# Attention and mixture-of-experts kernel: the softmax division moved from the probabilities to each pair's output, with an fp32 output product

## The reference

```
q = l2norm(q) * q_scale
k = l2norm(k) * k_scale
sim = einsum('bhid,bhjd->bhij', q, k) * SCALE + slopes * bias
sim = where(causal, -neg, sim)
attn = softmax(sim, axis=-1)
out = einsum('bhij,bhjd->bhid', attn, v)
out = out.transpose(0, 2, 1, 3).reshape(b, n, h * dh)
return out @ Wout
```

## Time and profile before

| | us |
|---|---|
| median of 3 runs (550.72 to 552.13) | 552.09 |
| the profiled execution, its own time | 550.33 |
| its span, from the first to the last instruction | 548.2 |
| start of step 4 of batch 0 / of batch 1 | 194.30 / 237.82 |
| one batch of the loop, step 4 to step 4 | 45.88 to 45.90 |
| step 4 of batch 6 to that of batch 7 | 44.08 |
| step 4 of batch 7 to the end | 36.86 |

### The profile page before, as it was taken

How to read it: one execution, slowest core, us unless ns; L and a number is a source line. 1 busy time by engine, 2 the same in 40 slices (tenths; PEclk the granted TensorE clock), 3 DMA queues, 4 the chain that set the end, 5 groups by cost and what they waited for, 6 DMA issues and landing times.

```text
span 548.2 us, 12299 instructions
## 1 busy us (share of the span) xinstructions
PE 431.0 (79%) x2867; PEld 318.0 (58%) x2868; DVE 413.8 (75%) x1468; ACT 365.9 (67%) x1097; POOL 320.1 (58%) x488
## 2 busy tenths in 40 slices
PE   0573334987889788997998998899799889889885
PEld 0472222766667566765765765576576566667663
DVE  3865713554455289989889998898899899899885
ACT  1451214565556687895886888689588788868864
POOL 2223778940000278957867886795886788678140
PEclk9996757799999999998998999999899999989999
DMA  8930111222221100000000100100000010010010
GB/s 220 352 109 21 48 43 54 57 60 59 61 62 57 31 0 15 8 1 21 21 0 10 29 0 0 29 10 0 19 19 0 4 34 0 0 29 10 3 39 10
DMA packets 28586, 21.17 MB, mean 39 GB/s; under 512 B 3560, under 2 KB 25744, under 8 KB 28432
## 3 DMA queue, kind: packets, MB, share of 16 engines
q1 hardware_dynamic: 25696, 16.65, 10.3%
q0 software_dynamic: 2048, 4.20, 2.5%
q10 hardware_dynamic: 816, 0.03, 0.1%
HBM read 12.48 MB, written 8.39 MB: 38 GB/s over the span
## 4 chain that ended last, share of the span: by engine, by line
POOL 29%; issue 22%; PE 20%; DVE 17%; ACT 4%; DMA 3%; POOLq 1%; SPq 1%; DVEq 1%; ACTq 0%
POOL rnorm L418 6%; POOL slot_x L408 6%; POOL arena_b L498 5%; POOL rpow L421 5%; PE bank L945 4%; DVE arena_b L894 3%; DVE arena_b L878 3%; PE bank L1152 3%; POOL pnull L487 3%; PE bank L947 3%; PE bank L946 3%; DMA arena_b<-in_L_ffn_wu_dram 2%; PE bank L1123 2%; PE bank L1131 2%; PE bank L1076 2%
## 5 line engine op out<-in xcount | busy, mean ns | idle before, releaser
L652 ACT ACTIVATE arena_b<-arena_b,nmx 128x130 f32<-128x130 f32 (+1 forms) x256 | 115.2, 458 | 29.3 <-DVE nmx L894 20.3
L878 DVE TENSOR_SCALAR arena_b<-arena_b,rden 128x130 f32<-128x130 f32 (+1 forms) x256 | 104.6, 454 | 4.6
L894 DVE CUSTOM_DVE_ANT_0 arena_b<-bank,bias 128x130 f32<-128x130 f32 (+1 forms) x256 | 81.0, 354 | 17.1 <-PE bank L1076 9.1
L1076 PE MATMUL bank<-arena_a 64*128 64x130 f32 (+1 forms) x512 | 59.7, 352 | 23.7 <-DVE nmx L894 22.7
L421 POOL TENSOR_TENSOR rpow<-ssm,mhalf 128x8 f32<-128x8 f32 x32 | 52.8, 1649 | 40.6 <-DVE ssm L859 40.6
L1067 PE MATMUL bank<-ident,arena_b 128*128 128x128 f32 x384 | 67.2, 284 | 7.0 <-DVE arena_b L878 7.0
L434 POOL TENSOR_TENSOR arena_b<-arena_b,rnorm 128x512 f32<-128x512 f32 x64 | 67.1, 1048 | 8.4 <-POOL rnorm L424 3.8
L590 ACT ACTIVATE arena_b<-bank 128x512 f32<-128x512 f32 x64 | 38.2, 597 | 32.0 <-PE bank L947 31.3
L418 POOL TENSOR_TENSOR rnorm<-ssm,mhalf 128x8 f32<-128x8 f32 x32 | 52.4, 1639 | 7.6 <-DVE ssm L859 7.6
L855 DVE TENSOR_REDUCE ssq<-arena_b 128x8 f32<-128x512 f32 x64 | 43.4, 678 | 16.0 <-ACT arena_b L590 15.9
L1076 PEld LDWEIGHTS bank<-arena_a 64*128 64x128 f32 x512 | 33.6, 186 | 36.5 <-DVE nmx L894 30.5
(11 more groups left out here) (203 smaller groups left out, 1128.1 us busy)
## 6 DMA issues: line engine op xcount, KB each, us to landing
slot_x<-probT SPq DMA_DIRECT2D x4, 640.0 KB, 7.7
arena_b<-slot_x SPq DMA_DIRECT2D x40, 64.0 KB, 1.8
slot_y<-arena_b SPq DMA_DIRECT2D x40, 64.0 KB, 1.6
arena_b<-in_L_ffn_wd_dram SPq DMA_DIRECT2D x1, 1024.0 KB, 10.3
arena_b<-in_L_attn_Wkv_dram SPq DMA_DIRECT2D x1, 1024.0 KB, 8.5
arena_b<-in_L_attn_x_dram SPq DMA_DIRECT2D x8, 128.0 KB, 2.1
out_dram<-arena_b SPq DMA_DIRECT2D x8, 128.0 KB, 1.8
arena_b<-in_L_attn_Wq_dram SPq DMA_DIRECT2D x1, 512.0 KB, 6.4
```

The lines of the kernel that those rows point to most:

```text
L652: sc.activation(prob[:, h % 4, c], sim[h % 2][:, c], ACT.Exp, scale=-1.0, bias=nmx[:, h % HEADS, t:t + 1], accum_out=den[:, h % HEADS, t:t ...
L878: ve.tensor_scalar(pr, pr, rden[:, h % HEADS, t:t + 1], None, ALU.mult).then_inc(g.pn, 1)
L894: ve.tensor_tensor_reduce(out=sim[h % 2][:, c], in0=bank[h % 2][:, c], in1=bias[:, c], scale=-SLOPES[h], scalar=3e38, op0=ALU.add, op1=ALU ...
L1076: ins = te.matmul(bank[half][:, c0:c1], qT[r, h // 2, q0:q0 + P], kT[r, h // 2, 0:c1 - c0], start=True, stop=True)
```

## The change

The probabilities stay as the exponential leaves them. For each pair of heads (odd h):

- DVE takes one reciprocal for both heads, in step h+2, and no longer multiplies (16 reciprocals and 32 multiplications of a batch become 8 reciprocals).
- POOL, in step h+2 and behind the norms of that step, spreads the reciprocals of the pair over a 128x256 tile `rwide`. It then multiplies the null columns by them where it copied before.
- PE, in step h+3 and behind the transposes of the probabilities, waits for it (`rw`) and transposes `rwide` into `rpair`, the other half of bank 4. It waits there for `odone` of the pair before as well.
- ACT, in step h+3, copies `rpair` to `rows` (it no longer reads `opair` in step h+5).
- DVE, in step h+5, multiplies `opair` by `rows` into `oT` (fp32).
- PE, in step h+6, uses one fp32 product in place of three fp32r products. `wo` is loaded as it is, its split in the prologue goes.

The diff, cut to its core:

```diff
@@ POOL, entry
                     if h is not None and h % 2:
                         p = h // 2
-                        pool.wait_ge(g.pn, TB * (HEADS * b + h + 1))
+                        pool.wait_ge(g.rd, PAIRS * b + p + 1)
+                        if part != "first" or p >= 2:
+                            pool.wait_ge(g.rps, PAIRS * b + p - 1)
+                        settled(pool)
+                        gp.tensor_copy(rwide[p % 2][:].rearrange("p (t h d) -> p t h d", t=TB, d=DH),
+                                       rden[:, 2 * (p % PAIRS):2 * (p % PAIRS) + 2, :].rearrange("p h t -> p t h").unsqueeze(3)
+                                       .to_broadcast([P, TB, 2, DH])).then_inc(g.rw, 1)
...
-                            gp.tensor_copy(pnull[:, t, 4 * q:4 * q + 4].rearrange("p (h n) -> p h n", n=2),
-                                           two[:, :, c0:c0 + NNULL]).then_inc(g.pnc, 1)
+                            gp.tensor_tensor(pnull[:, t, 4 * q:4 * q + 4].rearrange("p (h n) -> p h n", n=2),
+                                             two[:, :, c0:c0 + NNULL], bc(rden[:, 2 * q:2 * q + 2, t], NNULL),
+                                             ALU.mult).then_inc(g.pnc, 1)
@@ ACT, entry
-                    h = head_at(part, s, 5)
-                    if h is not None and h % 2:
-                        p = h // 2
-                        act.wait_ge(g.pvd, PAIRS * b + p + 1)
-                        if part != "first" or p >= 2:
-                            act.wait_ge(g.oread, PAIRS * b + p - 1)
-                        sc.activation(oT[p % 2][0], opair, ACT.Copy).then_inc(g.ohi, 1)
                     for job in behind(part, b, s, 1):
                         side_out(*job)
                     h = head_at(part, s, 3)
                     if h is not None and h % 2 == 1:
+                        p = h // 2
+                        act.wait_ge(g.rps, PAIRS * b + p + 1)
+                        if part != "first" or p >= 2:
+                            act.wait_ge(g.odone, PAIRS * b + p - 1)
+                        sc.activation(rows[p % 2][:], rpair, ACT.Copy).then_inc(g.rev, 1)
@@ DVE, entry
-                        dve.wait_ge(g.ohi, PAIRS * b + p + 1)
-                        ve.tensor_tensor(oT[p % 2][1], opair, oT[p % 2][0].bitcast(F32),
-                                         ALU.subtract).then_inc(g.olo, 1)
+                        dve.wait_ge(g.pvd, PAIRS * b + p + 1)
+                        dve.wait_ge(g.rev, PAIRS * b + p + 1)
+                        if part != "first" or p >= 2:
+                            dve.wait_ge(g.oread, PAIRS * b + p - 1)
+                        ve.tensor_tensor(oT[p % 2][:], opair, rows[p % 2][:], ALU.mult).then_inc(g.odone, 1)
                     h = head_at(part, s, 2)
-                    if h is not None:
+                    if h is not None and h % 2:
                         dve.wait_ge(g.exp, TB * (HEADS * b + h + 1))
-                        ve.reciprocal(rden[:, h % HEADS, :], den[:, h % HEADS, :]).then_inc(g.rd, 1)
-                        dve.wait_ge(g.rd, HEADS * b + h + 1)
-                        for t, c in ((0, slice(0, K0)), (1, slice(K0, KS))):
-                            pr = prob[:, h % 4, c]
-                            ve.tensor_scalar(pr, pr, rden[:, h % HEADS, t:t + 1], None, ALU.mult).then_inc(g.pn, 1)
+                        hh = slice((h - 1) % HEADS, (h - 1) % HEADS + 2)
+                        ve.reciprocal(rden[:, hh, :], den[:, hh, :]).then_inc(g.rd, 1)
@@ PE, entry
-                        if part != "first" or p >= 1:
-                            pe.wait_ge(g.olo, PAIRS * b + p)
+                        pe.wait_ge(g.rev, PAIRS * b + p + 1)
...
-                        pe.wait_ge(g.pn, TB * (HEADS * b + h + 1))
+                        pe.wait_ge(g.exp, TB * (HEADS * b + h + 1))
...
                         ins.then_inc(g.ptps, 1)
+                        if h % 2:
+                            p = h // 2
+                            pe.wait_ge(g.rw, PAIRS * b + p + 1)
+                            if part != "first" or p >= 1:
+                                pe.wait_ge(g.odone, PAIRS * b + p)
+                            for t in range(TB):
+                                ins = te.transpose(rpair[:, t * P:(t + 1) * P], rwide[p % 2][:, t * P:(t + 1) * P], ident[:])
+                            ins.then_inc(g.rps, 1)
...
-                        pe.wait_ge(g.olo, PAIRS * b + p + 1)
-                        three(bank[6][:, 0:SEQ], [x[:, p % PAIRS, :] for x in wo], oT[p % 2], p == 0,
-                              p == -1).then_inc(g.oread, 1)
+                        pe.wait_ge(g.odone, PAIRS * b + p + 1)
+                        te.matmul(bank[6][:, 0:SEQ], wo[:, p % PAIRS, :], oT[p % 2][:], start=p == 0,
+                                  stop=p == -1).then_inc(g.oread, 1)
```

More of the change, by code:

```diff
@@ L62, in build @@
         wkv = [sb("wkv_hi", [P, 2 * INNER], F32R), sb("wkv_lo", [P, 2 * INNER], F32R)]
-        wo = [sb("wo_hi", [P, PAIRS, DIM], F32R), sb("wo_lo", [P, PAIRS, DIM], F32R)]
+        wo = sb("wo", [P, PAIRS, DIM])
         sgu = [sb("sgu_hi", [P, 2 * I], F32R), sb("sgu_lo", [P, 2 * I], F32R)]
@@ L99, in build @@
         raw_w = carve(3 * INNER)
-        raw_o = carve(PAIRS * DIM).rearrange("p (c d) -> p c d", d=DIM)
         assert at[0] <= 11008
@@ L134, in build @@
         rt[0] = 4 * SEQ
-        oT = [[carve_r(SEQ), carve_r(SEQ)] for _ in range(2)]
+        oT = [sb(f"oT{i}", [P, SEQ]) for i in range(2)]
+        rows = [sb(f"rows{i}", [P, SEQ]) for i in range(2)]
+        rwide = [sb(f"rwide{i}", [P, SEQ]) for i in range(2)]
         hss = [carve_r(2 * I), carve_r(2 * I)]
-        opair = bank[4][:, 0:SEQ]
+        opair, rpair = bank[4][:, 0:SEQ], bank[4][:, SEQ:2 * SEQ]
         pnT = sb("pnT", [96, SEQ], F32R)
@@ L202, in build @@
             "sh_th", "sh_a", "sh_h", "sh_hi", "sh_lo", "shd",
-            "sps", "ttr", "exp", "rd", "pn", "ptps", "ptev_a", "ptev_d", "pvd", "ohi", "olo", "oread",
+            "sps", "ttr", "exp", "rd", "ptps", "ptev_a", "ptev_d", "pvd", "rw", "rps", "rev", "odone", "oread",
             "pnc", "pn_hi", "pn_lo", "yev", "zc", "fin", "stored", "res_in", "gath", "passed", "now",
@@ L327, in _ @@
             sync.dma_start(raw_w[:, INNER:3 * INNER], a["L0_attn_Wkv"]).then_inc(g.w_in, 16)
-            sync.dma_start(raw_o, a["L0_attn_Wout"].rearrange("(c p) d -> p c d", p=P)).then_inc(g.o_in, 16)
+            sync.dma_start(wo[:], a["L0_attn_Wout"].rearrange("(c p) d -> p c d", p=P)).then_inc(g.o_in, 16)
             sync.wait_ge(g.nvz, 1)
@@ L335, in _ @@
             sync.wait_ge(g.scattered, 16 * NT * TOPK)
-            sync.wait_ge(g.wraw_lo, 3)
+            sync.wait_ge(g.wraw_lo, 2)
             def turn(it, first, drain, steps=range(MU)):
@@ L552, in _ @@
             sc.activation(lth, lg, ACT.Tanh, scale=0.5).then_inc(g.lth_ready, 1)
-            act.wait_ge(g.o_in, 16)
             sc.activation(wkv[0][:], raw_w[:, INNER:3 * INNER], ACT.Copy).then_inc(g.wraw_hi, 1)
-            sc.activation(wo[0][:], raw_o, ACT.Copy).then_inc(g.wraw_hi, 1)
             act.wait_ge(g.small_in, 16 * 9)
@@ L808, in _ @@
                 split_group(n)
-            dve.wait_ge(g.wraw_hi, 3)
+            dve.wait_ge(g.wraw_hi, 2)
             ve.tensor_tensor(wq[1][:], raw_w[:, 0:INNER], wq[0][:].bitcast(F32), ALU.subtract).then_inc(g.wraw_lo, 1)
             ve.tensor_tensor(wkv[1][:], raw_w[:, INNER:3 * INNER], wkv[0][:].bitcast(F32), ALU.subtract).then_inc(g.wraw_lo, 1)
-            ve.tensor_tensor(wo[1][:], raw_o, wo[0][:].bitcast(F32), ALU.subtract).then_inc(g.wraw_lo, 1)
             dve.sem_inc(g.fin, 1)
@@ L993, in _ @@
             for p in range(PAIRS):
-                ins = te.matmul(bank[7][0:32, 256:256 + DIM], nvT[:, 32 * p:32 * p + 32], raw_o[:, p, :],
+                ins = te.matmul(bank[7][0:32, 256:256 + DIM], nvT[:, 32 * p:32 * p + 32], wo[:, p, :],
                                 start=p == 0, stop=p == PAIRS - 1)
@@ L1001, in _ @@
             pe.wait_ge(g.w_lo, len(groups))
-            pe.wait_ge(g.wraw_lo, 3)
+            pe.wait_ge(g.wraw_lo, 2)
             pe.wait_ge(g.un_ready, 1)
```

## The result

The changed kernel takes 595.96 us (median; 593.95 to 598.33) against 552.11 us for the kernel before (550.72 to 553.56) on the same chip: ratio 1.080, interval 1.074 to 1.085. The forecast was 584 us, range 563 to 602. The direction and the mechanism held; the loss was 43.9 us where I had worked out 31.5.

A forecast was written before the change was run, and what follows sets the result against it. DVE was taken as the bound, to be replaced by a POOL-PE ring. Terms 19.3 + 5.7 + 3.8 + 2.2 + 0.5 = 31.5 us on 550.33 gave 581.8; median forecast 584 us, range 563 to 602.

The forecast's parts named there:

- Step 1: From PE's scores of step 4 to POOL's start on the norm of that step's kq job: 3.56 us, unchanged.
- the ring: PE's even-step scores wait for POOL's `rw`; POOL's norms wait for DVE's sums, queued behind PE: period 49.7 us against 45.88.
- Step 2: POOL from that norm to `rw` of step 11: 21.42 us plus 2.0 for four widenings, so `rw` at 27.0 us.
- Step 3: PE from `rw` of step 11 to the scores of step 4 of the next batch: 22.7 us.
- Step 4: The period of a batch, 27.0 + 22.7 = 49.7 us against 45.88.
- last batch: From step 4 of batch 7, scores of step 12 come at 532.4 against 530.18: +2.2 us.
- The signs named: PE idles 2 us or more at steps 8 and 12; POOL's sum waits fall from 7.2 us; POOL near 38.
- A: Rival: DVE was the bound and PE takes over, faster; period 44.1 us, time 539 us; chance 0.08.
- B: Rival: POOL's instructions get shorter with L878 gone; period 46.7 us, time 562 us; chance 0.12.
- C: Rival: PE's stalls cost more than themselves, through half clock and slower widening; up to 4 us a period, 605; chance 0.1.
- D: Rival: the ring closes elsewhere, for instance over ACT; 1 us a period more, 591 us; chance 0.10.
- The rule weighed: GpSimd shares SBUF interfaces with VectorE; read as DVE paying for contention, so POOL gains nothing from L878's removal.

The follow-up runs named there:

- e3: Changed kernel, but PE transposes a tile of ones without waiting for POOL's widening, which POOL still does: 549.66 us, 0.996 of the kernel before.
- e2: Changed kernel with the widening copy into `rwide` done on DVE behind the reciprocal instead of on POOL: 549.13 us, 0.995 of the kernel before.
- e6: e2 with DVE's multiplication of the output one step earlier, ahead of the copy to `probT` and the odd scores: 536.83 us, 0.971 of the kernel before.
- e7: Changed kernel with POOL's four gathers moved from step 10 to behind the widening of step 11: 625.73 us, 1.133 of the kernel before.
- e1: Changed kernel with POOL's widening written ahead of the norms of its step, nothing else: 579.16 us, 1.051 of the kernel before.

## Why the prediction was right, and where it was short

**DVE was the bound and stops being it**: right. Its 41.35 us became 29.89, not about 26. L878's groups were gone as said. But the 14.5 us taken off for them were count times mean duration, and these instructions overlap: the row's busy time of 104.6 us is 13.1 a batch. And others got longer: in the batch shown L850 rose from 1.4 to 2.2 us busy and L861 from 1.4 to 2.6 (below).

**Step 1 of the ring** (3.56 us): 3.55.

**Step 2, `rw` of step 11 at 27.0 us**: 27.6 (423.52 + 0.40 - 396.28). The widening was priced too high, 0.36 to 0.40 instead of 0.50, which is 0.4 to 0.6 us over four. The wait of 1.58 us for the sums of step 7's job was said to go "since POOL will be further behind". 1.41 of it stayed. DVE's timeline shows what stands in front of that sum:

```profile
408.86 0.41 DVE L843 TENSOR_TENSOR arena_b<-bank,arena_b 128x256 f32<-128x256 f32 x1
409.44 2.26 DVE L850 SCALAR_TENSOR_TENSOR arena_b<-arena_b,w_now 128x128 f32<-128x128 f32 x4 [0.17 <-DVE arena_b L843]
411.62 0.68 DVE L857 TENSOR_REDUCE ssq<-arena_b 128x8 f32<-128x512 f32 x1
412.42 0.17 DVE L861 TENSOR_SCALAR ssm<-ssq 128x8 f32<-128x8 f32 x1
```

The gathered rows are weighed (L850) ahead of the sum, and the four took 2.26 us where the same four (L848) took 1.45 before (at 390.06). A later POOL doesn't shorten a wait whose source is held by the same ring: PE stalls, DVE's sums move with PE, and POOL is late and waits too.

**Step 3, 22.7 us from `rw` to the next step 4**: 22.9 (423.92 to 446.86). The fp32 product took 401.89 - 401.46 = 0.43 us, the price of the three fp32r products that it replaces, not 0.53.

**Step 4, a period of 49.7 us**: 50.58 in this batch, 50.76 over five (244.24 to 498.03). The difference in this batch is the 0.6 us of step 2 and the 0.2 of step 3; two of the five had half clock besides (50.90 and 51.17 us at a mean of 0.97, the others 50.55 to 50.59 at 1.00).

**The sum**, forecast against measured: head +0.5 and +1.2; batch 0 to 1 +5.7 and +5.2; five periods +19.3 and +24.4; batch 6 to 7 +3.8 and +6.7; last batch +2.2 and +6.4. Together +31.5 and +43.9. The five periods are short by 5.1 us: 4.2 from steps 2 and 3 of the ring and 0.9 from the half clock. Two terms of the ends were mis-sized. *Batch 6 to 7*: the kq job that is missing after step 13 saved 1.8 us before and saved 0.4 now (446.86 - 424.35 = 22.51 against 548.80 - 526.71 = 22.09), and the stretch from step 4 to step 12 was 0.6 longer at half clock. *The last batch*: up to step 12 it lost 2.5 us, as the forecast's +2.2 says. Behind it I had counted nothing, and it lost 4.0 us more (592.10 - 570.12 = 22.0 against 18.0). PE's timeline there:

```profile
569.76 0.44 PE L1075 MATMUL bank<-ident,rwide 128*128 128x128 f32 x2 [2.58 <-POOL rwide L485]
```

The window behind it:

```profile
570.00:575.00 5.00, 5.00 (x30) 3.88 (x29) 2.24 (x11) 2.62 (x10) 0.72 (x4) 0.66 0.05 13
```

The waits of the last batch (548.80 to 592.10):

```profile
POOL rwide L485 <- DVE rden L879: 18.8, 6, 5.0
ACT rows L640 <- PE bank L1075: 14.3, 8, 3.2
...
PE bank L1075 <- DVE oT L874: 2.9, 4, 1.1
```

POOL and ACT wait long here because their inputs come late, and that costs nothing by itself. PE stalls once for POOL, 2.58 us, and then runs 5 us at a mean clock of 0.66. The scores of step 14 (start, us), before and after:

```profile
533.81 0.93 PE L1076 MATMUL bank<-arena_a 64*128 64x130 f32 x8
```

```profile
575.62 0.93 PE L1084 MATMUL bank<-arena_a 64*128 64x130 f32 x8
```

From the scores of step 12 to these it is 5.5 us against 3.6 before, 1.9 lost. e3 has the new work without the wait and without the slow clock there and takes 4.2 (526.79 to 530.97), so new work is 0.6 of the 1.9. The other 1.3 go with the stretch at half clock, which can cost at most 1.7. From step 14 to the end it is 16.5 us against 14.4, 2.1 lost. Here POOL's copy has no part: e2 needs the same 16.5 (from 531.60) and e3 16.4 (from 530.97), neither waiting for POOL. e6, which differs from e2 by the earlier multiplication of the output, needs 14.9 (from 521.04). So these 2.1 us are the longer chain from exponential to output, in a stage in which nothing else hides it, and 1.6 of them hang on the place of DVE's multiplication. The prediction had the ring and left out this chain.

**The signs named.** PE's transposes of step 8 idled 1.98 to 2.46 us for POOL, as said. Those of step 12 idled 1.83 to 1.85 in three of the five mid batches, and only 0.61 and 0.91 in the two with a stretch at half clock ahead of them. POOL's waits for the sums were to fall from 7.2 us and are 7.5: 4.38 of them stand ahead of the norm of step 4, where the ring runs through PE and POOL has nothing to do. POOL at 37.1 us is near the 38 named.

**The rivals.** A (539 us) did not come, for the reason given: POOL's lateness is its own. e2 and e6 show that A is what the change gives once POOL is out of the way. B (POOL's instructions get shorter) is refuted: L435 took 1041, 1042 and 1045 ns at least, in the median and at most. Before, seven of the 64 L434 took 1083 to 1118 ns, each begun while an L878 was running; that is 0.3 us in all. C was part of the truth and smaller than feared: a mid batch with a stretch at half clock was 0.3 to 0.6 us longer (50.90 and 51.17 against 50.57), since PE's stall of step 12 shrank from 1.83 us to 0.61 and 0.91 and took up the rest; at the last batch it was 1.3. D: no wait for ACT closed the ring.

**The rule weighed** stands as it was read. The Trainium skill (GPSIMD Engine Reference, Key points) names contention between GpSimd and VectorE instructions with two SBUF inputs. The trace agrees, and shows that DVE pays in the changed kernel: L850, with two such inputs, took 346 to 352 ns each at 588.6 us, with POOL idle, and up to 1217 ns beside POOL, while POOL's L435 stayed at 1042.

## What to carry to other kernels

Before a small step goes to an engine that looks free, follow what each engine that reads it does next. If the reader runs in order and feeds the writer, the two form a ring, and the step costs its place in the writer's queue, not its duration: 64 copies of 0.4 us cost 46 us here, and the same copies on DVE, behind their producer, cost none of it (e2). Busy shares (POOL at 58%) say nothing on this; the lateness of one engine's timeline against the other's does, and it must be laid out for the whole turn, since moving one item (e7) can lose what it wins at another place.

## What the runs showed of the hardware that I had not expected

**Some DVE instructions that fall on a POOL operation of two inputs end only when POOL's does.** They are L850, which reads two tiles in SBUF, and L861, which takes the maximum of a tiny tile and a constant; before, L878 was another (up to 1143 ns). In the changed kernel POOL's L435 ran from 409.46 to 410.50. DVE's first L850 began at 409.44 and took 1208 ns, to 410.65; the last two of the four took 352 and 346. The tiny L861 (8 elements a partition, 172 ns in the median) took 608 ns at 402.38, up to 402.99, beside the L435 that ended at 402.96. At 407.18 it took 404, up to 407.58, beside POOL's L463, which ran from 406.83 to 407.57. In e1, where the order differs, L850 has a mean of 349 ns; in the changed kernel 534. Other DVE instructions beside the same L435 kept their time: the reduction L857 took 0.68 us at 401.58, with L435 from 401.92 on, and 0.68 at 411.62 with none; L827, which reads one input from PSUM, took 0.42 us in the midst of an L435 (at 414.85), as without one. Four L850 stand in a batch ahead of a sum that POOL waits for, 2.26 us against 1.26 with POOL idle (at 588.62), so this is up to 1.0 us of each turn of the ring. That it closes the ring tighter is worked out from these rows; no kernel was made to test it alone.

**The clock falls at some stalls of PE, in them or behind them.** Behind 2.2 to 4.1 us of idle PE, stretches of 4 to 5 us ran at a mean of 0.60 to 0.66 of the full clock, that is for the most part at 1.2 GHz. In e7 the clock was at half already during a stall of 4.07 us, which ended at 231.81:

```profile
229.95:231.75 1.80, 0.00 (x0) 0.00 (x0) 0.00 (x0) 0.00 (x0) 1.72 (x4) 0.50 0.00 0
```

The kernel before has such stretches too, behind waits of 1.4 us, and they cost it nothing (45.88 us at a mean of 0.96, 45.89 at 1.00). And not each stall did it: behind the 2.19 us at 410.96 in the batch shown the clock stayed at 1.00, and behind 2.20 us at 512.71 it fell:

```profile
512.71 0.44 PE L1075 MATMUL bank<-ident,rwide 128*128 128x128 f32 x2 [2.20 <-POOL rwide L485]
513.08 1.66 PE L1084 MATMUL bank<-arena_a 64*128 64x130 f32 x8
```

The same scores take 0.93 us elsewhere. What tells the two apart was not found.
